# Token rows transposed by copies in SBUF and VectorE blocks instead of TensorE, in a fused attention and mixture-of-experts kernel

## The chip, the cores and the metric

The kernel runs on one core of one Trainium2 chip. The metric is the device time of one launch in microseconds. Three runs of the kernel before gave 1381.59 us as their median (1374.52 to 2207.56).

## The reference, cut to what matters

The input `x` has 4 x 2048 = 8192 tokens of 512 features. All arithmetic is float32.

```
xn  = layernorm(x)                                   # per token, no scale
attn: feats   = exp(xis * (xn @ proj.T) - ...)       # random features, 512 of them
      weights = the same of input_weights            # 512 x 512, made once
      attn    = feats @ weights.T
moe:  score = sigmoid(xn @ router_w)                 # 64 experts
      best 4 of 8 groups, then the best 8 experts, weights normalised, times 2.5
      each expert takes its first 256 tokens: silu(t @ gate) * (t @ up) @ down
      shared expert: silu(xn @ sgate) * (xn @ sup) @ sdown
out = x + attn + moe
```

Every product over the 512 features needs the tokens with features along the partitions, so each group of rows has to be transposed once.

## The kernel before, in words

**Stages.** The kernel has a start (about the first 60 us), a dense stage that goes over 16 groups of 512 tokens, and an expert stage that goes over 64 experts. A float32 product is made of three fp32r matmuls (high times high, low times high, high times low; lines 1034 to 1036), so every operand exists as a high and a low half.

**Start.** SyncE (SP) issues nearly all loads in one queue. Lines 389 to 403 load `xis`, `proj`, `input_weights`, the rows of group 0, the router and the shared expert's gate and up matrices. The last three go through `load_shifted` (lines 333 to 339), which loads a matrix shifted by one row, in three DMAs: three blocks of 128 rows, 127 rows, and one row. VectorE (DVE) then waits for `shared_loaded` (line 922), subtracts the first row from all rows (line 923), and goes on with the low halves, the moments of group 1 and the scores of group 0. TensorE (PE) takes up group 0 behind these.

**Dense stage.** In group g, PE makes 48 matmuls of random features (`dense_dots`), 48 of the shared expert's gate and up, 8 of the next group's router logits, and 72 for the output, in the order of `group` at line 1149. Between them it transposes the next group's normalised rows `xn` in two halves of 8 transposes (`turn_half`, line 1039) into the PSUM tile `ptr`. ScalarE (ACT) copies each half to `xt_hi` (`hi_half`), DVE makes `xt_lo` (`lo_half`). In group g DVE also finds the deviations and normalises group g + 1, and takes the moments of group g + 2 between the outputs 1 and 2 of group g.

**What sets the order.** Each engine's program is written out by hand and waits on semaphores; nothing is planned by a scheduler. SP's order in a group is that of `group` at line 377: the residual rows of group g, x of group g + 2, the store of `xn` of group g + 1 to the table `rows`, then the first half of the output, the router weights and counts of group g + 1, and the second half of the output. A residual is loaded only after the output that lay in the same tile has landed (line 370). The weights of experts 0 and 1 are loaded during the start into `raw[1]` and `raw[0]`.

Of the kernel before, what the change touches and what calls it, by code (L numbers as in the profile page):

```python
# [26 lines left out]
P = 128  # L27
H = 512
# [17 lines left out]
SLOTS = E * CAP  # L46
SPARE = CAP
ROW = H + E
GU = 2 * HB * I
# [38 lines left out]
def build(nc, x, iw, xis, proj, router_w, gate_w, up_w, down_w, sgate_w, sup_w, sdown_w, out):  # L88
    with ExitStack() as ctx:
# [98 lines left out]

        router_raw = gate_a[:, 0:HB * E].rearrange("p (c e) -> p c e", c=HB)
        square = hid  # L190
        iw_raw = raw[1][:, 0:HB * (H + 1)].rearrange("p (c d) -> p c d", c=HB)
# [58 lines left out]
        norm_made = sem("norm_made")  # L250
        xn_stored = sem("xn_stored")
        w_made = sem("w_made")
        w_stored = sem("w_stored")
# [55 lines left out]
        x_groups = x.rearrange("b s h -> (b s) h").rearrange("(g j p) h -> g p j h", j=J, p=P)  # L309
        x_halves = x.rearrange("b s h -> (b s) h").rearrange("(g a j p) h -> g a p j h", a=2, j=2, p=P)  # L310
        rows_groups = rows[0:TOKENS, :].rearrange("(g j p) h -> g p j h", j=J, p=P)
        out_halves = out[0:TOKENS, :].rearrange("(g a j p) h -> g a p j h", a=2, j=2, p=P)
# [9 lines left out]
        def _(sp):  # L322
            def load_x(g):
                sp.dma_start(xbuf[g.b][:], x_groups[g.n]).then_inc(x_loaded[g.b], 16)

            def load_gate_up(b, gate, up):

                sp.dma_start(raw[b][:, 0:GU // 2], gate.rearrange("(p c) i -> p (c i)", p=P)).then_inc(
                    gu_loaded[b], 16)
                sp.dma_start(raw[b][:, GU // 2:GU], up.rearrange("(p c) i -> p (c i)", p=P)).then_inc(  # L330
                    gu_loaded[b], 16)

            def load_shifted(place, source, loaded):
# [14 lines left out]
            def store_xn(g):  # L348
                sp.wait_ge(xn_made, g.n + 1)
                sp.dma_start(rows_groups[g.n][:, :, 0:H], xn[:, :, 0:H]).then_inc(xn_stored, 16)  # L350

            def store_w(g):
# [23 lines left out]

            def group(g, load=True, last=False):
# [6 lines left out]
                if not last:  # L384
                    store_w(g.next())
                    store_counts(g.next())
                store_out(g, 1)
# [25 lines left out]
            sp.wait_ge(iw_sums_turned, 1)  # L413
            load_gate_up(1, gate_w[1], up_w[1])
            load_down(1, down_w[1])
            store_xn(turn(0))
            sp.wait_ge(shared_lo_made, 2)
            load_gate_up(0, gate_w[0], up_w[0])
            load_down(0, down_w[0])
            sp.wait_ge(table_made, 16 * (1 + 2 * SPARE // P))  # L420
# [3 lines left out]
            sp.wait_ge(router_less_made, 1)  # L424
            group(turn(0))
# [4 lines left out]
            group(turn(GROUPS - 2), load=False)  # L430
            load_residual(turn(GROUPS - 1))
# [34 lines left out]
        def _(act):  # L466
# [32 lines left out]
            def hi_half(n, half, dst, psum=ptr):  # L499

                act.wait_ge(turned, 2 * n + half + 1)
                act.activation(dst[:, 2 * half:2 * half + 2, :], psum[:], copy).then_inc(xt_hi_made, 1)

            def sum_signs(n):
# [10 lines left out]
            def group(g, last=False):  # L515
                nxt = g.next()
                for r in range(HB):
                    features(1 + g.n, r, feat_hi)
                if not last:
                    hi_half(nxt.n + 2, 0, xt_hi[nxt.b])  # L520
                hidden(g, 0)
                if not last:
                    hi_half(nxt.n + 2, 1, xt_hi[nxt.b])
# [49 lines left out]
            act.activation(sdn_hi[:], raw[0][:, GU:], copy).then_inc(shared_hi_made, 1)  # L573
            group(turn(0))
            group(turn(1))
# [71 lines left out]
        def _(dve):  # L647
# [23 lines left out]
            def lo_half(n, half, hi, lo, psum=ptr):  # L671
# [3 lines left out]
                    xt_lo_made, 1)  # L675

            def features_lo(s, r, hi, lo, scale=1.0):
                dve.wait_ge(feat_hi_made, HB * s + r + 1)
# [8 lines left out]
            def moments(g):  # L687

                dve.wait_ge(x_loaded[g.b], 16 * (g.i + 1))
                for j in range(J):  # L690
# [23 lines left out]
            def normalise(g, base):  # L714

                dve.wait_ge(turned, 2 * (g.n + 2))
                at_least(dve, xn_stored, 16 * g.n)
                for j in range(J):
# [109 lines left out]
            def group(g, base, before_last=False, last=False):  # L828
# [3 lines left out]
                if not last:  # L832
                    deviations(nxt, base)
                features_lo(1 + g.n, 1, feat_hi, feat_lo)
                if not last:
                    normalise(nxt, base)
                features_lo(1 + g.n, 2, feat_hi, feat_lo)
                features_lo(1 + g.n, 3, feat_hi, feat_lo)
                if last:
                    pass_blocks(0)  # L840
                else:
# [6 lines left out]
            def outputs(g, base, before_last=False, last=False):  # L848

                nxt = g.next()  # L850
                if not last:
# [85 lines left out]
            def first_group(g, base):  # L937
# [11 lines left out]
                weigh(g, base)  # L949
                lo_half(nxt.n + 2, 1, xt_hi[nxt.b], xt_lo[nxt.b])  # L950
                hidden(g, 0, base)
                hidden_lo(g, 0)
# [15 lines left out]
            steps[0] = 0  # L968
            group(turn(GROUPS - 2), start + per_group * (GROUPS - 2), before_last=True)
            steps[0] = 0  # L970
            group(turn(GROUPS - 1), start + per_group * (GROUPS - 1), last=True)

# [57 lines left out]
        def _(pe):  # L1030
# [8 lines left out]
            def turn_half(n, src, half, psum=ptr, free=None):  # L1039
# [3 lines left out]
                for h in range(2):  # L1043
                    for j in range(J):
                        at = 1 + (2 * half + h) * P
                        ins = pe.transpose(psum[:, h, j * P:(j + 1) * P], src[:, j, at:at + P], ident[:])  # L1046
                ins.then_inc(turned, 1)
# [101 lines left out]
            def group(g):  # L1149
                nxt = g.next()  # L1150
                first = isinstance(g.n, int) and g.n == 0
                dense_dots(g, range(1 if first else 0, HB))
                pe.wait_ge(xn_made, nxt.n + 1)
                turn_half(nxt.n + 2, xn, 0)
                if first:
                    pe.wait_ge(shared_lo_made, 1)
                shared_products(g, 0, 0)
                pe.wait_ge(norm_made, nxt.n + 1)
                turn_half(nxt.n + 2, xn, 1)
                if first:  # L1160
                    count(g)
                shared_products(g, 0, 1)
# [34 lines left out]
            pe.transpose(ppos[:, 0:HB], xis_row[:], ident[0:HB, 0:HB]).then_inc(xis_turned, 1)  # L1197
            pe.wait_ge(proj_copied, 1)
            turn_half(0, xn, 0, free=0)
            pe.wait_ge(proj_copied, 2)  # L1200
# [3 lines left out]
            pe.wait_ge(iw_loaded[0], 16)  # L1204
            turn_half(1, iw_raw, 0, psum=pout2, free=0)
            pe.wait_ge(iw_loaded[1], 16)
            pe.wait_ge(pads_made, 1)
            turn_half(1, iw_raw, 1, free=1)
# [11 lines left out]
            for r in range(2, HB):  # L1220
                pe.wait_ge(exp_done, r - 1)
                if r == HB - 1:
                    pe.wait_ge(xn_made, 1)
                    turn_half(2, xn, 0, psum=pout2, free=3)
                    pe.wait_ge(norm_made, 1)
                    turn_half(2, xn, 1, free=4)
# [76 lines left out]
        def _(pool):  # L1303
# [84 lines left out]
            pool.wait_ge(slot_cols_made, 1)  # L1388
            pool.wait_ge(xn_stored, 16 * GROUPS)
            pool.wait_ge(w_stored, 16 * GROUPS)  # L1390
# [40 lines left out]
```

## Time and profile before

| | |
|---|---|
| median of three runs | 1381.59 us |
| time of the profiled execution | 1388.1 us |
| its span, from the first to the last instruction | 1386.4 us |
| mean granted TensorE clock | 0.989 of full speed |
| PE busy | 1333.4 us (96%) |
| DVE busy | 862.1 us (62%) |
| ACT busy | 639.9 us (46%) |
| POOL busy | 480.3 us (35%) |

How to read it: the span is cut into the start, the dense stage (to about 750 us) and the expert stage. A share of busy time is a mean over all three. PE's busy time comes from matmuls that overlap in the trace; the distance between the starts of two of them is what one costs.

### The profile page before, as it was taken

What the parts mean: (1) busy time and instruction counts of PE and PEld (TensorE: products, weight loads), DVE (VectorE), ACT (ScalarE), POOL (GpSimd) and SP (SyncE); (2) the same over time, 40 slices, a digit from 0 to 9 for tenths busy, and PEclk for the clock granted to TensorE, in tenths of its full rate; (3) what the DMA queues carried; (4) which work ended last, traced back from release to release, by engine and by line L of the source; (5) the groups of instructions that cost most, each with busy time, mean ns of one, the idle gap of its engine ahead of it and who ended that gap; (6) DMA issues with size and microseconds to landing.
All of it is one profiled execution on the core that took longest, in us unless ns stands there. A gap on an engine that the chain in (4) does not pass through costs nothing.

```text
span 1386.4 us, 22484 instructions
## 1 busy us (share of the span) xinstructions
PE 1333.4 (96%) x7837; PEld 1165.6 (84%) x7837; DVE 862.1 (62%) x1661; ACT 639.9 (46%) x988; POOL 480.3 (35%) x347
## 2 busy tenths in 40 slices
PE   6899999999999999999999999999999999999994
PEld 5688888888888888888888999999999999888884
DVE  7865755657556575565636676666766666656551
ACT  5311232212322123221236777777777776765662
POOL 1200000000000000000004676877777777555643
PEclk9899999999999999999999999999999999999997
DMA  6351333312333123331217999999999999999895
GB/s 209 128 202 58 106 110 127 108 59 105 107 127 111 61 102 107 127 115 62 68 54 241 263 292 284 280 285 281 288 290 276 295 277 278 260 256 257 240 251 66
DMA packets 117501, 250.00 MB, mean 180 GB/s; under 512 B 31450, under 2 KB 34782, under 8 KB 117470
## 3 DMA queue, kind: packets, MB, share of 16 engines
q1 hardware_dynamic: 88798, 178.28, 38.2%
q0 software_dynamic: 28672, 71.32, 22.7%
q8 instruction: 17, 0.28, 0.1%
q14 instruction: 14, 0.11, 0.0%
HBM read 178.18 MB, written 71.39 MB: 180 GB/s over the span
## 4 chain that ended last, share of the span: by engine, by line
PE 52%; DMA 27%; POOL 9%; issue 6%; DVE 2%; SPq 2%; ACT 1%; DVEq 0%; POOLq 0%; ACTq 0%
DMA out_dram<-outs,slot_cols 24%; PE pmm L1034 9%; PE pmm L1036 9%; PE pmm L1035 9%; POOL out_dram L1383 8%; PE pout L1034 7%; PE pout L1036 6%; PE pout L1035 6%; DMA xbuf<-rows,slot_cols 2%; PE ptr L1046 2%; PE plog L1095 2%; POOL xbuf L1373 2%; SPq L339 1%; PE plog L1104 1%; PE ptr L1249 1%
## 5 line engine op out<-in xcount | busy, mean ns | idle before, releaser
L1383 POOL DMA_INDIRECT out_dram<-outs,slot_cols x128 | 253.3, 1979 | 162.3 <-DMA out_dram<-outs,slot_cols 128.2
L1034 PE MATMUL pmm<-xt_hi,proj_hi 128*128 128x256 f32 (+1 forms) x784 | 253.5, 323 | 4.4 <-DVE xt_lo L989 2.3
L1034 PE MATMUL pmm<-xt_hi,sgu_hi 128*128 128x256 f32 (+1 forms) x768 | 253.1, 330 | 0.0
L1036 PE MATMUL pmm<-xt_hi,proj_lo 128*128 128x256 f32 (+1 forms) x784 | 250.0, 319 | 0.0
L1035 PE MATMUL pmm<-xt_lo,proj_hi 128*128 128x256 f32 (+1 forms) x784 | 250.0, 319 | 0.0
L1036 PE MATMUL pmm<-xt_hi,sgu_lo 128*128 128x256 f32 (+1 forms) x768 | 246.4, 321 | 0.0
L1035 PE MATMUL pmm<-xt_lo,sgu_hi 128*128 128x256 f32 (+1 forms) x768 | 246.2, 321 | 0.0
L1367 POOL TENSOR_TENSOR earlier<-earlier,chosen 128x64 bf16<-128x64 bf16 x64 | 28.6, 446 | 612.0 <-DVE chosen L759 608.2
L1373 POOL DMA_INDIRECT xbuf<-rows,slot_cols x128 | 185.0, 1445 | 91.2 <-DVE slot_cols L802 38.1
L473 ACT ACTIVATE feat<-pmm,ab 128x512 f32<-128x512 f32 x68 | 46.8, 688 | 317.1 <-PE pmm L1036 309.0
L1034 PEld LDWEIGHTS pmm<-xt_hi,proj_hi 128*128 128x128 f32 x784 | 148.3, 189 | 16.1 <-DVE xt_lo L989 2.8
L1036 PEld LDWEIGHTS pmm<-xt_hi,proj_lo 128*128 128x128 f32 x784 | 149.5, 191 | 10.7
L1035 PEld LDWEIGHTS pmm<-xt_lo,proj_hi 128*128 128x128 f32 x784 | 148.1, 189 | 10.5
L1036 PEld LDWEIGHTS pmm<-xt_hi,sgu_lo 128*128 128x128 f32 x768 | 145.9, 190 | 10.9
L1034 PEld LDWEIGHTS pmm<-xt_hi,sgu_hi 128*128 128x128 f32 x768 | 146.5, 191 | 8.8 <-issue 0.2
L1035 PEld LDWEIGHTS pmm<-xt_lo,sgu_hi 128*128 128x128 f32 x768 | 146.1, 190 | 8.9
L983 DVE COPY slot_w<-xbuf 128x2 f32 (+1 forms) x64 | 12.1, 189 | 163.2 <-ACT xt_hi L595 151.8
L612 ACT ACTIVATE outs<-pout,slot_w 128x512 f32<-128x512 f32 x128 | 85.5, 684 | 42.2 <-PE pout L1036 29.5
L1034 PE MATMUL pout<-sdn_hi,hid_hi 128*128 128x512 f32 x256 | 101.4, 396 | 0.0
L1034 PE MATMUL pout<-wt_hi,feat_hi 128*128 128x512 f32 x256 | 101.2, 395 | 0.0
L1036 PE MATMUL pout<-wt_hi,feat_lo 128*128 128x512 f32 x256 | 99.8, 390 | 0.0
L1036 PE MATMUL pout<-sdn_hi,hid_lo 128*128 128x512 f32 x256 | 99.8, 390 | 0.0
(180 smaller groups left out, 2563.5 us busy)
## 6 DMA issues: line engine op xcount, KB each, us to landing
raw<-in_L_ffn_gate_w_dram SPq DMA_DIRECT2D x64, 512.0 KB
raw<-in_L_ffn_up_w_dram SPq DMA_DIRECT2D x64, 512.0 KB
raw<-in_L_ffn_down_w_dram SPq DMA_DIRECT2D x64, 512.0 KB
xbuf<-in_L_attn_x_dram SPq DMA_DIRECT2D x16, 1024.0 KB, 6.4
rows<-xn SPq DMA_DIRECT2D x16, 1024.0 KB, 4.2
outs<-in_L_attn_x_dram SPq DMA_DIRECT2D x32, 512.0 KB, 3.6
out_dram<-outs SPq DMA_DIRECT2D x32, 512.0 KB, 2.9
rows<-weight SPq DMA_DIRECT2D x16, 128.0 KB, 2.8
```

Source lines behind the costliest of these rows:

```text
L339: sp.dma_start(place[P - 1:P, HB - 1], source[0:1]).then_inc(loaded, 16)
L473: act.activation(feat[:, r % 2], pmm[r % 2], ACT.Exp, scale=ab[:, r:r + 1]).then_inc(exp_done, 1)
L612: act.activation(outs[e.b][:, c], pout[c], copy, scale=slot_w[e.q][:, c:c + 1]).then_inc(e_out_made, 1)
L1034: pe.matmul(psum, lh, rh, start=first and n == 0, stop=False)
L1035: pe.matmul(psum, lh, rl, start=False, stop=False)
L1036: ins = pe.matmul(psum, ll, rh, start=False, stop=final and n == len(pairs) - 1)
L1046: ins = pe.transpose(psum[:, h, j * P:(j + 1) * P], src[:, j, at:at + P], ident[:])
L1095: ins = pe.matmul(plog[:], router[:, h, :], part[g.b][:, h, :], start=(h == 0 and part is xt_hi), stop=(h == HB - 1 and part is xt_lo))
L1104: ins = pe.matmul(plog[:, j * E:(j + 1) * E], logits_t[:, j * P:(j + 1) * P], fold[:], start=True, stop=True)
L1367: pool.tensor_tensor(after, earlier[b][:, j, :], chosen[:, j, :], ALU.add).then_inc(earlier_made, 1)
L1373: pool.indirect_dma_start(out=xe[e.b][:, c, :], out_offset=None, in_=rows, in_offset=bass.IndirectOffsetOnAxis(ap=slot_cols[:, at:at + 1], ...
L1383: pool.indirect_dma_start(out=out, out_offset=bass.IndirectOffsetOnAxis(ap=slot_cols[:, at:at + 1], axis=0), in_=outs[e.b][:, c, :], in_of ...
```

## The change

For groups 2 to 15 PE no longer transposes. Instead:

- x is loaded in four DMAs, so that partition 4t + q holds tokens t, t + 32, t + 64 and t + 96 of quarter q of the group (`load_x_quads`). The store of `xn` is in four DMAs in the same way.
- Once group g + 2 is normalised, four DMAs copy `xn` within SBUF: block b of 128 features goes to the quarter of 32 partitions b of the tile `quad` (`load_quad`). A destination partition has 2048 numbers, made of 16 pieces of 128.
- DVE transposes blocks of 32 x 32 from `quad` to `xt_whole`, in two instructions of 1024 columns (`turn_quad`). ACT and DVE take the high and low halves from there.
- Deviations and normalisation of group g + 2 now stand in group g on DVE, between its outputs 1 and 2, and the moments of group g + 2 stand before `hidden(g, 0)`.
- A feature now lies at partition p, block c for feature 4p + c. `load_shifted` loads in that order: 127 partitions with four rows each, then three rows, then one. `turn_half`, still used for `proj`, `input_weights` and groups 0 and 1, reads every fourth column.
- `quad` and `xt_whole` lie in `raw[1]` and `raw[0]`, so the first two experts' weights are loaded in group 14 and no longer during the start.

```diff
 def load_shifted(place, source, loaded):
-    full = (HB - 1) * P
-    sp.dma_start(place[:, 0:HB - 1], source[1:1 + full].rearrange("(c p) i -> p c i", p=P)).then_inc(
+    full = (P - 1) * HB
+    sp.dma_start(place[0:P - 1], source[1:1 + full].rearrange("(p c) n -> p c n", c=HB)).then_inc(loaded, 16)
+    sp.dma_start(place[P - 1:P, 0:HB - 1], source[1 + full:].rearrange("(p c) n -> p c n", p=1)).then_inc(
         loaded, 16)
-    sp.dma_start(place[0:P - 1, HB - 1], source[1 + full:]).then_inc(loaded, 16)
     sp.dma_start(place[P - 1:P, HB - 1], source[0:1]).then_inc(loaded, 16)
...
+def load_x_quads(g):
+    for q in range(P // SQ):
+        sp.dma_start(xbuf[g.b][q:P:P // SQ], x_quads[g.n, q]).then_inc(x_loaded[g.b], 16)
+def load_quad(g):
+    sp.wait_ge(xn_made, g.n + 1)
+    sp.wait_ge(norm_made, g.n + 1)
+    at_least(sp, quad_turned, 2 * (g.n - 2))
+    for b in range(HB):
+        sp.dma_start(quad[b * SQ:(b + 1) * SQ, :], xn[:, :, 1 + b * P:1 + (b + 1) * P]).then_inc(
+            quad_loaded, 16)
...
     load_residual(g)
-    if load:
-        load_x(Turn(g.i + 1, g.b))
-    if not last:
-        store_xn(g.next())
+    if first:
+        store_xn(nxt)
+    else:
+        load_x_quads(later)
     store_out(g, 0)
...
+    store_w(nxt)
+    store_counts(nxt)
+    load_quad(later)
+    store_xn_quads(later)
     store_out(g, 1)
...
+def turn_quad(g, half):
+    dve.wait_ge(quad_loaded, 16 * HB * (g.n - 1))
+    at_least(dve, xt_hi_made, 2 * (g.n - 1 + 2) + 2)
+    at = slice(2 * half, 2 * half + 2)
+    dve.transpose(xt_whole[:, at, :].rearrange("p c (k i) -> p c k i", i=SQ),
+                  quad_blocks[:, at]).then_inc(quad_turned, 1)
...
     features_lo(1 + g.n, 0, feat_hi, feat_lo)
     if not last:
-        deviations(nxt, base)
+        turn_quad(nxt, 0)
+        turn_quad(nxt, 1)
     features_lo(1 + g.n, 1, feat_hi, feat_lo)
     if not last:
-        normalise(nxt, base)
+        lo_quad(nxt, 0)
     features_lo(1 + g.n, 2, feat_hi, feat_lo)
+    if not last:
+        lo_quad(nxt, 1)
     features_lo(1 + g.n, 3, feat_hi, feat_lo)
...
-        lo_half(nxt.n + 2, 0, xt_hi[nxt.b], xt_lo[nxt.b])
-        lo_half(nxt.n + 2, 1, xt_hi[nxt.b], xt_lo[nxt.b])
+    elif not before_last:
+        moments(Turn(g.i + 1, g.b))
     hidden(g, 0, base)
...
-        moments(Turn(g.i + 1, g.b))
+        deviations(later, base)
+        normalise(later, base)
     output(g, 2)
...
     dense_dots(g, range(1 if first else 0, HB))
-    pe.wait_ge(xn_made, nxt.n + 1)
-    turn_half(nxt.n + 2, xn, 0)
     if first:
+        pe.wait_ge(xn_made, nxt.n + 1)
+        pe.wait_ge(norm_made, nxt.n + 1)
+        turn_half(nxt.n + 2, xn, 0)
         pe.wait_ge(shared_lo_made, 1)
     shared_products(g, 0, 0)
-    pe.wait_ge(norm_made, nxt.n + 1)
-    turn_half(nxt.n + 2, xn, 1)
     if first:
+        turn_half(nxt.n + 2, xn, 1)
         count(g)
```

The first place is SP's queue in the start, from the rows of group 0 on (`gate_a` holds the raw router, `raw` the raw shared matrices). Before:

```order
L324 DMA xbuf<-in_L_attn_x_dram 128x4x512
L336 DMA gate_a<-in_L_ffn_router_w_dram 128x3x64
L338 DMA gate_a<-in_L_ffn_router_w_dram 127x64
L339 DMA gate_a<-in_L_ffn_router_w_dram 1x64
L397 DMA outs<-in_L_ffn_router_w_dram 128x64
L336 DMA raw<-in_L_ffn_shared_gate_w_dram 128x3x256
L338 DMA raw<-in_L_ffn_shared_gate_w_dram 127x256
L339 DMA raw<-in_L_ffn_shared_gate_w_dram 1x256
L336 DMA raw<-in_L_ffn_shared_up_w_dram 128x3x256
L338 DMA raw<-in_L_ffn_shared_up_w_dram 127x256
L339 DMA raw<-in_L_ffn_shared_up_w_dram 1x256
L401 DMA outs<-in_L_ffn_shared_gate_w_dram 128x256
```

The same place in the changed kernel:

```order
L332 DMA xbuf<-in_L_attn_x_dram 128x4x512
L349 DMA gate_a<-in_L_ffn_router_w_dram 127x256
L350 DMA gate_a<-in_L_ffn_router_w_dram 1x192
L352 DMA gate_a<-in_L_ffn_router_w_dram 1x64
L439 DMA outs<-in_L_ffn_router_w_dram 128x64
L349 DMA raw<-in_L_ffn_shared_gate_w_dram 127x1024
L350 DMA raw<-in_L_ffn_shared_gate_w_dram 1x768
L352 DMA raw<-in_L_ffn_shared_gate_w_dram 1x256
L349 DMA raw<-in_L_ffn_shared_up_w_dram 127x1024
L350 DMA raw<-in_L_ffn_shared_up_w_dram 1x768
L352 DMA raw<-in_L_ffn_shared_up_w_dram 1x256
L443 DMA outs<-in_L_ffn_shared_gate_w_dram 128x256
```

The number of DMAs is the same; the 127-partition DMA has four times the data, and the 128-partition one is gone.

The second place is SP's queue at the end of a group inside the loop, from the counts on. Before, the output's second half follows them at once:

```order
L359 DMA counts_d<-counts 64x2x128
L374 REGISTER_ALU
L375 DMA out_dram<-outs 128x2x512
L85 REGISTER_ALU
L371 ISA
L371 DMA outs<-in_L_attn_x_dram 128x2x512
```

In the changed kernel:

```order
L385 DMA counts_d<-counts 64x2x128
L367 REGISTER_ALU
L86 ISA
L371 DMA raw<-xn 32x16x128 x4
L376 ISA
L376 DMA rows<-xn 32x4x512
L376 ISA
L376 DMA rows<-xn 32x4x512
...
L400 REGISTER_ALU
L401 DMA out_dram<-outs 128x2x512
```

Eight DMAs, 2 MB in all, stand between the counts and the output's second half (two of the four pairs of L376 are left out here).

## Rows read from the trace of the kernel before

**Rows 1.** Windows: PE, PEld, DVE, ACT, POOL busy us (count); PEclk, DMA share, GB/s.

```profile
90.00:650.00 560.00, 559.85 (x2644) 460.35 (x2643) 345.78 (x935) 138.68 (x208) 23.41 (x52) 1.00 0.30 102
```

**Rows 2.** Timeline of PE in one dense group: start us, us, instruction.

```profile
394.46 0.39 PE L1034 MATMUL pmm<-xt_hi,proj_hi 128*128 128x512 f32 x1
...
405.11 0.39 PE L1036 MATMUL pmm<-xt_hi,proj_lo 128*128 128x512 f32 x1
405.35 1.03 PE L1046 MATMUL ptr<-ident,xn 128*128 128x128 f32 x8
...
406.45 0.40 PE L1035 MATMUL pmm<-xt_lo,sgu_hi 128*128 128x512 f32 x1
...
408.73 0.39 PE L1036 MATMUL pmm<-xt_hi,sgu_lo 128*128 128x512 f32 x1
...
410.29 0.39 PE L1035 MATMUL pmm<-xt_lo,sgu_hi 128*128 128x512 f32 x1
...
414.65 0.39 PE L1034 MATMUL pmm<-xt_hi,sgu_hi 128*128 128x512 f32 x1
...
437.72 0.39 PE L1034 MATMUL pmm<-xt_hi,proj_hi 128*128 128x512 f32 x1
```

**Rows 3.** Chain that ended last, the start stage: start us, us, what.

```profile
24.25 5.76 DMA outs<-n_L_ffn_shared_up_w_dram
...
62.00 0.53 PE pmm L1034
```

**Rows 4.** Timeline of DVE in the start; in brackets the idle time before it.

```profile
30.03 2.29 DVE L669 TENSOR_TENSOR raw<-raw,outs 128x2048 f32<-128x2048 f32 x1 [2.18 <-DMA outs<-n_L_ffn_shared_up_w_dram]
```

**Rows 5.** Timeline of SP in the start: start us, us in its queue.

```profile
6.42 6.10 SPq L339 DMA_DIRECT2D gate_a<-in_L_ffn_router_w_dram  x1
...
18.54 5.27 SPq L339 DMA_DIRECT2D raw<-n_L_ffn_shared_up_w_dram  x1
```

**Rows 6.** Windows of the start, columns as in Rows 1.

```profile
21.80:23.60 1.80, 1.19 (x5) 0.45 (x4) 1.49 (x11) 0.86 (x2) 0.00 (x0) 1.00 0.07 24
48.50:50.50 2.00, 2.00 (x11) 1.65 (x10) 1.97 (x4) 0.70 (x2) 0.00 (x0) 1.00 1.02 414
```

**Rows 7.** Timeline of DVE in the same dense group.

```profile
399.46 0.18 DVE L698 BATCH_NORM_AGGREGATE mean_var<-stats 128x2 f32<-128x6 f32 x1
...
402.06 0.16 DVE L711 SCALAR_TENSOR_TENSOR rstd<-rstd 128x4 f32<-128x4 f32 x1
...
402.95 1.91 DVE L719 TENSOR_SCALAR xn<-xbuf,mean_var,rstd 128x512 f32<-128x512 f32 x4
...
407.84 1.23 DVE L674 TENSOR_TENSOR xt_lo<-ptr,xt_hi 128x1024 fp32r<-128x1024 f32 x1 [0.22 <-ACT xt_hi L502]
...
413.17 0.69 DVE L813 SCALAR_TENSOR_TENSOR hid<-gate_a,pmm 128x512 f32<-128x512 f32 x1
...
430.04 0.41 DVE L777 TENSOR_SCALAR counts<-ppos 128x256 bf16<-128x256 f32 x1
430.37 2.46 DVE L691 BATCH_NORM_STATS2 stats<-xbuf 128x6 f32<-128x512 f32 x4
```

**Rows 8.** Timeline of ACT in the same group.

```profile
402.82 0.69 ACT L473 ACTIVATE feat<-pmm,ab 128x512 f32<-128x512 f32 x1 [1.37 <-PE pmm L1036]
```

**Rows 9.** Timeline of SP at the group's end.

```profile
439.29 2.96 SPq L371 DMA_DIRECT2D outs<-in_L_attn_x_dram  x2
442.44 0.37 SPq L324 DMA_DIRECT2D xbuf<-in_L_attn_x_dram  x1
```

**Rows 10.** Page, part 6: DMA issues, KB each, median us from issue to landing.

```profile
xbuf<-in_L_attn_x_dram SPq DMA_DIRECT2D x16, 1024.0 KB, 6.4
rows<-xn SPq DMA_DIRECT2D x16, 1024.0 KB, 4.2
...
out_dram<-outs SPq DMA_DIRECT2D x32, 512.0 KB, 2.9
rows<-weight SPq DMA_DIRECT2D x16, 128.0 KB, 2.8
```

More of the change, by code:

```diff
@@ L310, in build @@
         x_halves = x.rearrange("b s h -> (b s) h").rearrange("(g a j p) h -> g a p j h", a=2, j=2, p=P)
+        x_quads = x.rearrange("b s h -> (b s) h").rearrange("(g q j t) h -> g q t j h", q=P // SQ, j=J, t=SQ)
+        rows_quads = rows[0:TOKENS, :].rearrange("(g q j t) h -> g q t j h", q=P // SQ, j=J, t=SQ)
         rows_groups = rows[0:TOKENS, :].rearrange("(g j p) h -> g p j h", j=J, p=P)
@@ L350, in store_xn, with store_xn_quads @@
                 sp.dma_start(rows_groups[g.n][:, :, 0:H], xn[:, :, 0:H]).then_inc(xn_stored, 16)
+            def load_quad(g):
[5 more added lines that the diff above has]
+                        quad_loaded, 16)
+            def store_xn_quads(g):
+                for q in range(P // SQ):
+                    sp.dma_start(rows_quads[g.n, q][:, :, 0:H], xn[q:P:P // SQ, :, 0:H]).then_inc(xn_stored, 16)
             def store_w(g):
@@ L375, in store_out, with group, before_last_group @@
                 sp.dma_start(out_halves[g.n, a], outs[a][:]).then_inc(out_stored[a], 16)
-            def group(g, load=True, last=False):
+            def group(g, first=False):
+                nxt, later = g.next(), Turn(g.i + 1, g.b)
                 load_residual(g)
-                if load:
-                    load_x(Turn(g.i + 1, g.b))
-                if not last:
-                    store_xn(g.next())
+                if first:
+                    store_xn(nxt)
+                else:
+                    load_x_quads(later)
                 store_out(g, 0)
-                if not last:
-                    store_w(g.next())
-                    store_counts(g.next())
+                store_w(nxt)
+                store_counts(nxt)
+                load_quad(later)
+                store_xn_quads(later)
+                store_out(g, 1)
+            def before_last_group(g):
+                nxt = g.next()
+                load_residual(g)
+                sp.wait_ge(quad_turned, 2 * (GROUPS - 2))
+                load_gate_up(1, gate_w[1], up_w[1])
+                load_down(1, down_w[1])
+                sp.wait_ge(xt_lo_made, 2 * (GROUPS + 2))
+                load_gate_up(0, gate_w[0], up_w[0])
+                load_down(0, down_w[0])
+                store_out(g, 0)
+                store_w(nxt)
+                store_counts(nxt)
                 store_out(g, 1)
@@ L424, in _ @@
             sp.wait_ge(router_less_made, 1)
-            group(turn(0))
+            group(turn(0), first=True)
             group(turn(1))
@@ L429, in _ @@
                     group(Turn(i, b))
-            group(turn(GROUPS - 2), load=False)
+            before_last_group(turn(GROUPS - 2))
             load_residual(turn(GROUPS - 1))
@@ L502, in hi_half, with hi_quad @@
                 act.activation(dst[:, 2 * half:2 * half + 2, :], psum[:], copy).then_inc(xt_hi_made, 1)
+            def hi_quad(g, half):
+                act.wait_ge(quad_turned, 2 * (g.n - 2) + half + 1)
+                act.wait_ge(up_done, IB * (g.n - 1))
+                at = slice(2 * half, 2 * half + 2)
+                act.activation(xt_hi[g.b][:, at, :], xt_whole[:, at, :], copy).then_inc(xt_hi_made, 1)
             def sum_signs(n):
@@ L513, in sum_signs, with group @@
                     ins.then_inc(signs_summed, 1)
-            def group(g, last=False):
+            def group(g, first=False, last=False):
                 nxt = g.next()
-                for r in range(HB):
-                    features(1 + g.n, r, feat_hi)
-                if not last:
+                features(1 + g.n, 0, feat_hi)
+                features(1 + g.n, 1, feat_hi)
+                if not first and not last:
+                    hi_quad(nxt, 0)
+                features(1 + g.n, 2, feat_hi)
+                if not first and not last:
+                    hi_quad(nxt, 1)
+                features(1 + g.n, 3, feat_hi)
+                if first:
                     hi_half(nxt.n + 2, 0, xt_hi[nxt.b])
                 hidden(g, 0)
-                if not last:
+                if first:
                     hi_half(nxt.n + 2, 1, xt_hi[nxt.b])
@@ L573, in _ @@
             act.activation(sdn_hi[:], raw[0][:, GU:], copy).then_inc(shared_hi_made, 1)
-            group(turn(0))
+            group(turn(0), first=True)
             group(turn(1))
@@ L714, in normalise @@
             def normalise(g, base):
-                dve.wait_ge(turned, 2 * (g.n + 2))
-                at_least(dve, xn_stored, 16 * g.n)
+                if isinstance(g.n, int) and g.n <= 2:
+                    dve.wait_ge(turned, 2 * (g.n + 2))
+                    at_least(dve, xn_stored, 16 * g.n)
+                else:
+                    dve.wait_ge(quad_loaded, 16 * HB * (g.n - 2))
+                    dve.wait_ge(xn_stored, 32 + 16 * (P // SQ) * (g.n - 2))
                 for j in range(J):
@@ L848, in outputs @@
             def outputs(g, base, before_last=False, last=False):
-                nxt = g.next()
+                nxt, later = g.next(), Turn(g.i + 1, g.b)
                 if not last:
@@ L950, in first_group @@
                 lo_half(nxt.n + 2, 1, xt_hi[nxt.b], xt_lo[nxt.b])
+                moments(Turn(g.i + 1, g.b))
                 hidden(g, 0, base)
@@ L968, in _ @@
             steps[0] = 0
-            group(turn(GROUPS - 2), start + per_group * (GROUPS - 2), before_last=True)
+            start += per_group * (GROUPS - 2)
+            group(turn(GROUPS - 2), start, before_last=True)
+            start += steps[0]
             steps[0] = 0
-            group(turn(GROUPS - 1), start + per_group * (GROUPS - 1), last=True)
+            group(turn(GROUPS - 1), start, last=True)
             def down_lo(e):
@@ L1044, in turn_half @@
                     for j in range(J):
-                        at = 1 + (2 * half + h) * P
-                        ins = pe.transpose(psum[:, h, j * P:(j + 1) * P], src[:, j, at:at + P], ident[:])
+                        block = src[:, j, 1 + 2 * half + h::HB]
+                        ins = pe.transpose(psum[:, h, j * P:(j + 1) * P], block, ident[:])
                 ins.then_inc(turned, 1)
@@ L1203, in _ @@
             turn_six(less3).then_inc(less_turned, 1)
-            pe.wait_ge(iw_loaded[0], 16)
+            for half in range(2):
+                pe.wait_ge(iw_loaded[half], 16)
+            pe.wait_ge(pads_made, 1)
             turn_half(1, iw_raw, 0, psum=pout2, free=0)
-            pe.wait_ge(iw_loaded[1], 16)
-            pe.wait_ge(pads_made, 1)
             turn_half(1, iw_raw, 1, free=1)
```

28 lines of the change are left out of this document (17 added, 11 removed).

## The prediction

> **What bounds the kernel now.** I read the windows first, then PE's own timeline, then the chain and the queues of the start. In the dense stage PE is busy 559.85 of 560 us at the full granted clock, without a wait [rows 1]. So there every matmul or transpose taken from PE is a gain in full, as long as what replaces it keeps up. One group lasts 43.26 us, from the matmul that opens it at 394.46 us to the one at 437.72 [rows 2]. The expert stage behind it issues the same instructions before and after, and I leave it out. In the start it is another matter: DVE waits 2.18 us for the last load of the shared matrices, which lands at 30.03 us [rows 3, 4], and from there a chain of work, mostly DVE's, leads to the matmul at 62.00 us with which PE takes up group 0 in earnest [rows 3]. A later landing moves everything behind it by the same time.
>
> **The transposes (gain).** In rows 2 two matmuls of 0.23 us each lie between the start of L1036 at 405.11 and the start of L1035 at 406.45. That is 1.34 us, of which 0.46 are the matmuls; 0.88 belong to the 8 transposes and the changes to and from them. The second half: 410.29 - 408.73 - 0.46 = 1.10 us. Together 1.98 us per group. Groups 2 to 15 lose them, 14 groups: **-27.7 us**.
>
> **The loads of the start (loss).** The changed `load_shifted` moves 127 partitions x 4 rows in one DMA. What does a DMA of 127 partitions cost? Between 21.80 and 23.60 us, while SP stands in the next one-row DMA (18.54 us, 5.27 long [rows 5]) and the 127-row DMA of a shared matrix is under way, the DMA share is 0.07 and the rate 24 GB/s [rows 6]: one of sixteen engines, where 16 give 414 GB/s in the same start [rows 6]. So 127 partitions go through one engine. Bytes on it before: 127 x 256 B for the router and 2 x 127 x 1024 B for gate and up, 292.6 KB (thousands of bytes). After: 127 x 1024 B and 2 x 127 x 4096 B, 1170.4 KB. Off goes its sixteenth of the three-block loads (884.7 KB / 16 = 55.3 KB). Net 822.5 KB more, in order, on one engine. At 24 GB/s that is 34.3 us; at 414 / 16 = 25.9 GB/s, the rate with packets of 4 KB, 31.8 us. I take the second, since the new pieces have that size: **+31.8 us**. The landing moves from 30.0 to about 62 us, and PE's start of group 0 from 62 to about 94 us. Bounds: below, a gain of 2.2 us, if the DMA is spread over all engines after all (DVE's whole idle time there [rows 4]); above, 37 us, if the queue of SP, which stood 6.10 us and 5.27 us in one-row DMAs behind such loads [rows 5], also holds back the loads behind for one more such stop.
>
> The Trainium skill ("DMA: Bandwidth & Descriptors", section "Why a DMA increments its semaphore by 16 and not by 1") says that a DMA runs on the largest number of engines up to 16 that divides the slowest dimension of both sides, and names 127 partitions as a case of one. By that rule the two big loads stay on one engine, as in the sum; the trace agrees, with 24 GB/s. This rule speaks against the change.
>
> The other edits of the start cost nothing that shows: PE waits for both halves of `proj` and `input_weights` before it turns them (a microsecond or two), and the router's rows come later, both long before 62 us; without that cover they would be on DVE's chain. Six DMAs of expert weights, 3 MB, leave the start and come in group 14; SP has some 25 us there between the new waits and the first output, and the copies need about 8 us at 414 GB/s [rows 6]. The moments of group 2 (2.46 us [rows 7]) now stand before `hidden(0, 0)` on DVE, where in group 0 the up product is waited for anyway.
>
> **What replaces the transposes.** DVE gets two transposes of 1024 columns. The trace has none. A subtraction of 1024 columns takes 1.23 us [rows 7]; half of it if two elements went per cycle, twice it if the blocks need two passes. I take 1.23 each. They stand in the place of the deviations (399.46 to 402.22, 2.76 us [rows 7]), so DVE is not later there; with 2.46 each it would be 2.2 us later, which the 43 us of a group with 0.62 busy on DVE take in. ACT copies the two high halves between exponentials, where it idles 1.37 us [rows 8]; a copy of 1024 columns should take it no longer than DVE's subtraction, 1.23. Both cost nothing, with PE's wait for the exponential two steps later as cover.
>
> The critical part is the **DMA chain**. Set the next group's start at 437.72. DVE ends the counts at 430.45, then the deviations (2.76) and the normalisation (402.95 to 405.14, 2.19) end at 435.4 [rows 7]. Only then does SP issue four copies, four stores of `xn`, and the second output store, which stood right behind the counts before. All run in order on the same engines. From issue to landing 512 KB take 2.9 us and 1 MB 4.2 us [rows 10]: 1.3 us for 512 KB, with 1.6 us fixed. The 2048 pieces of 512 B of the copy have no row. By bytes alone they take 2.6 us; by the router weights' pieces of 256 B (512 of them in 2.8 - 1.6 = 1.2 us [rows 10]) 4.8 us. Middle 3.7. The output store then lands at 435.4 + 1.6 + 3.7 + 2.6 + 1.3 = 444.6, with 443.5 and 445.7 as ends. For that landing the next residual load waits, and behind it stands x of the group after. Before, that residual was issued at 441.85 [rows 9], and x landed at 442.44 + 6.4 = 448.8 [rows 9, 10], 7.0 us later. So x lands at 451.6 (450.5 to 452.7).
>
> Who needs it? DVE's moments now stand before `hidden`, 2.46 us, then two operations of 0.69 us and about 0.2 between them, 4.0 in all [rows 7]; PE needs their result where L1034 stood at 414.65 [rows 2], in the next group at 457.91, less 1.98 for the transposes: 455.9. So x may land at 451.9 at the latest. The middle fits by 0.3 us; at the upper end 0.8 us are lost in each of 13 groups, 10 us. I set down **+1 us**, and keep 0 to +10. The copies themselves land by 435.4 + 1.6 + 3.7 = 440.7, DVE wants them at 442.7: no wait.
>
> The Trainium skill (same page, section "Why small descriptors are slow (HBM only)") says that copies within SBUF don't suffer from small pieces as HBM does. By it the copy would be near its lower end, and x would be in time in every group; no run here shows it yet.
>
> **Sum.** 1388.1 (the profiled execution) - 27.7 + 31.8 + 1.0 = 1393.2. The median of the runs shown is 1381.6, 0.5% below that execution; the difference of +5.1 set on the median gives **1387 us**. Range of this case alone: 1378 to 1399.
>
> **The rivals.**
> 1. *x comes too late* (slower). If a piece of 512 B costs as much as one of 2 KB (2.6 us / 512 each), the copy takes 10.4 us instead of 3.7, x lands at 458.3, 6.4 us after the last moment, and 13 groups lose 83 us: 1470. It decides from a copy of 4.0 us on; each further microsecond costs 13. To be slower by over 2% (27.6 us) it takes a copy of about 5.8 us. For it: a margin of 0.3 us, and eight issues of SP in a row. Against: the 256 B stores, that give 4.8. Typical 1392 to 1425.
> 2. *The big loads don't clog one engine*, or something else waits there anyway (faster). Then only the gain is left: 1381.6 - 27.7 - 2.2 + 1 = 1353. For it: nothing in the rows but that the source is one unbroken run. Against: the 127-row load before also was one, at 24 GB/s.
> 3. *Nothing gained on PE*: the freed time turns up as a wait for the high halves on ACT, with the loss in the start kept: 1381.6 + 31.8 = 1413. The margins above speak against it.
>
> **Chances.** My forecast 0.60; rival 1 0.26 (0.18 of it under 1409, 0.08 above); rival 2 0.11; rival 3 0.03. A measurement of this kernel tells about 2%, 27.6 us, from no change, so faster means below 1354 and slower above 1409. Faster 0.09, within 2% 0.80, slower 0.11. The range leaves out rival 2 and the cases above 1409, some 2 in 10: 1366 to 1409.
>
> **What would show it.** PE's timeline in a steady group: 41.3 us from group to group and no idle row. Right for the start: the wait of DVE for the shared matrices ends near 62 us, with a window of some 40 us at 25 GB/s and share 0.06. Rival 1: idle PE with `hid` as releaser in each group, and idle DVE before the moments, released by x. Rival 2: the shared matrices there before 30 us. I am wrong on the whole if the dense stage speeds up by 27.7 us and the start does not grow, or if the copy takes over 4 us.

## The result, and the profile after

The changed kernel is slower: four runs gave a median of 1472.75 us (1445.34 to 1510.27), where four of the kernel before gave 1378.09. Executions of one kernel come in a faster and a slower state, whatever the kernel, and every ratio here compares the faster ones alone: it is 1.0585, with a 95% interval of 1.043 to 1.0739. The forecast was 1387 with a range up to 1409. The profiled execution took 1445.34 us, its span is 1443.6.

The page after: PE busy, the slices of PE and of its granted clock, and the DMA issues (KB each, median us to landing), to be read beside [rows 1, 10].

```profile
PE 1325.9 (92%) x7613; PEld 1157.8 (80%) x7613; DVE 913.1 (63%) x1689; ACT 636.3 (44%) x988; POOL 493.0 (34%) x347
...
PE   6299988899889988899899999999999999999995
...
PEclk9599989999999999999999999999999999999998
...
xbuf<-in_L_attn_x_dram SPq DMA_DIRECT2D x56, 256.0 KB, 3.9
raw<-xn SPq DMA_DIRECT2D x56, 256.0 KB, 6.2
rows<-xn SPq DMA_DIRECT2D x56, 256.0 KB, 7.2
```

PE has its 224 transposes fewer (7613 instead of 7837 matmuls), yet is no longer full in the dense stage (the 8s in its row), and a copy of 256 KB takes longer to land than 1 MB of `xn` did before.

Where the time went is read off best at the first transpose of the expert stage, the end of the dense one. Its line in the kernel before, then after (ns min/median/max, first and last start in us):

```profile
L1249 PE MATMUL ptr<-ident,xbuf x512: 270/283/421, 735.1 to 1348.1; 128*128 128x128 f32 x171
```

```profile
L1323 PE MATMUL ptr<-ident,xbuf x512: 270/283/386, 809.8 to 1407.7; 128*128 128x128 f32 x171
```

The dense stage ends at 809.8 instead of 735.1 us: +74.7. The expert stage, from there to the end of the span, has the same instructions and took 1386.4 - 735.1 = 651.3 us before and 633.8 here. In the other profiles it lies between 633 us (copy_halves) and 683 us (two_queues), and no run shows why. So whole times can differ by tens of us for a reason that lies behind the dense stage, and below I compare the end of the dense stage, in one profile per kernel.

**The start.** DVE's row after, for [rows 4], and SP's queue, for [rows 5]:

```profile
58.75 2.29 DVE L720 TENSOR_TENSOR raw<-raw,outs 128x2048 f32<-128x2048 f32 x1 [29.96 <-DMA outs<-n_L_ffn_shared_up_w_dram]
```

```profile
13.39 10.65 SPq L350 DMA_DIRECT2D raw<-L_ffn_shared_gate_w_dram  x1
...
25.01 12.56 SPq L350 DMA_DIRECT2D raw<-n_L_ffn_shared_up_w_dram  x1
37.61 6.95 SPq L352 DMA_DIRECT2D raw<-n_L_ffn_shared_up_w_dram  x1
```

```profile
25.50:37.00 11.50, 7.64 (x39) 5.72 (x37) 3.26 (x8) 4.14 (x6) 0.00 (x0) 0.96 0.07 28
```

The window (columns as in [rows 6]) shows a DMA share of one engine in sixteen, at 28 GB/s, while the big loads run; it stays so until SP gets on to the loads behind them at 44.60 us. The shared matrices land at 58.75 us instead of 30.03: +28.7.

**The dense stage.** PE in one group after, for [rows 2]; SP, DVE and a window of the same group:

```profile
404.00 0.39 PE L1109 MATMUL pmm<-xt_hi,proj_hi 128*128 128x512 f32 x1
...
415.98 0.50 PE L1109 MATMUL pmm<-xt_hi,sgu_hi 128*128 128x512 f32 x1 [0.95 <-ACT feat L511]
...
426.50 0.50 PE L1109 MATMUL pmm<-xt_hi,sgu_hi 128*128 128x512 f32 x1 [2.96 <-DVE hid L882]
...
449.69 0.39 PE L1109 MATMUL pmm<-xt_hi,proj_hi 128*128 128x512 f32 x1
```

```profile
350.56 1.53 SPq L385 DMA_DIRECT2D counts_d<-counts  x2
...
397.69 1.53 SPq L385 DMA_DIRECT2D counts_d<-counts  x2
402.02 2.77 SPq L371 DMA_DIRECT2D raw<-xn  x4
404.98 3.07 SPq L376 DMA_DIRECT2D rows<-xn  x4
408.25 0.45 SPq L401 DMA_DIRECT2D out_dram<-outs  x1
408.96 7.20 SPq L397 DMA_DIRECT2D outs<-in_L_attn_x_dram  x2
416.34 3.11 SPq L337 DMA_DIRECT2D xbuf<-in_L_attn_x_dram  x4
```

```profile
412.19 3.89 DVE L733 STREAM_TRANSPOSE raw<-raw 128x1024 f32<-128x1024 f32 x2 [3.12 <-DMA raw<-xn]
...
422.67 2.47 DVE L756 BATCH_NORM_STATS2 stats<-xbuf 128x6 f32<-128x512 f32 x4 [2.54 <-DMA xbuf<-in_L_attn_x_dram]
```

```profile
404.00:411.00 7.00, 7.00 (x32) 5.82 (x31) 1.39 (x2) 2.64 (x4) 0.00 (x0) 1.00 1.25 135
412.00:414.00 2.00, 2.00 (x11) 1.65 (x10) 1.81 (x1) 0.00 (x0) 0.00 (x0) 1.00 1.05 406
```

The group shown lasts 449.69 - 404.00 = 45.69 us, where 41.3 was forecast and 43.26 was the value before; the one ahead of it, from counts to counts, 397.69 - 350.56 = 47.13 us. The copies begin at 402.02 and run at 135 GB/s until 411, with all engines taken; at 412 the stores behind them run at 406 GB/s. Everything in SP's queue follows: the residual loads, the second of which waits for the output to land, keep SP for 7.20 us, x is issued at 416.34 and holds DVE until 422.67, `hid` is late, PE waits 2.96 us. A smaller wait of 0.95 us comes through the transposes and the exponential. By the waits table, from 130 to 700 us PE waits 37.8 us for `hid` and 10.3 us for `feat`, 12 times each:

```profile
PE pmm L1109 <- DVE hid L882: 37.8, 12, 4.9
PE pmm L1109 <- ACT feat L511: 10.3, 12, 0.9
```

Over the whole dense stage (100 to 760 us) it is 40.8 us in 13 groups for `hid` and 11.4 us in 14 groups for `feat`:

```profile
PE pmm L1109 <- DVE hid L882: 40.8, 13, 4.9
PE pmm L1109 <- ACT feat L511: 11.4, 14, 0.9
```

On top of the waits the clock's mean falls. Windows of the same stretch, before and then after (columns as in [rows 1]):

```profile
130.00:700.00 570.00, 569.83 (x2687) 468.59 (x2686) 345.57 (x935) 138.67 (x208) 23.41 (x52) 1.00 0.29 99
```

```profile
130.00:700.00 570.00, 521.92 (x2267) 423.44 (x2267) 367.21 (x892) 126.46 (x195) 19.24 (x48) 0.96 0.46 116
```

The granted clock goes from 1.00 to 0.96 in a stage whose PE now pauses. It does not fall after every pause. Windows of 1 us from 130 to 700 us show ten stretches at half clock (1.2 GHz), 41.0 us together, one at each of ten of the 13 waits for `hid`; the other three waits, that of the group shown among them, have none. One such stretch, behind a wait of 2.90 us that ended at 379.24, as a window and in PE's rows, where the starts lie 0.43 us apart instead of 0.23:

```profile
381.00:384.00 3.00, 3.00 (x11) 2.71 (x12) 1.02 (x2) 0.38 (x1) 0.00 (x0) 0.50 0.00 0
```

```profile
382.82 0.63 PE L1110 MATMUL pmm<-xt_lo,sgu_hi 128*128 128x512 f32 x1
383.25 0.63 PE L1111 MATMUL pmm<-xt_hi,sgu_lo 128*128 128x512 f32 x1
```

Later groups with such a stretch last 47.1 to 47.6 us from counts to counts, those without 45.6. One of the ten stretches is three times as long as the others and stands at the longest wait, 4.88 us; its group lasts 51.88 us. From these lengths I estimate the cost of the lower clock at some 19 us in all.

### The profile page after: what moved, and what is told of

Its sections match the earlier page's. It is cut to its first block, busy times and chain, and to the rows that moved or that the text cites. A ratio compares the mean times of both kernels' runs of the same rounds, so it can differ in the third digit from the quotient of the medians.

```text
span 1443.6 us, 22418 instructions
## 1 busy us (share of the span) xinstructions
PE 1325.9 (92%) x7613; PEld 1157.8 (80%) x7613; DVE 913.1 (63%) x1689; ACT 636.3 (44%) x988; POOL 493.0 (34%) x347
## 4 chain that ended last, share of the span: by engine, by line
DMA 34%; PE 27%; SPq 11%; DVE 10%; POOL 9%; issue 8%; ACT 1%; DVEq 0%; POOLq 0%; ACTq 0%
DMA out_dram<-outs,slot_cols 21%; POOL out_dram L1457 8%; DMA out_dram<-outs 7%; PE pmm L1109 5%; PE pmm L1111 4%; PE pmm L1110 4%; PE pout L1109 4%; PE pout L1111 4%; PE pout L1110 4%; DMA xbuf<-in_L_attn_x_dram 4%; SPq L376 3%; SPq L371 3%; SPq L350 2%; SPq L337 2%; DVE stats L756 2%
## 5 line engine op out<-in xcount | busy, mean ns | idle before, releaser
L1109 PE MATMUL pmm<-xt_hi,sgu_hi 128*128 128x256 f32 (+1 forms) x768 | 258.1, 336 | 52.2 <-DVE hid L882 40.8
L1457 POOL DMA_INDIRECT out_dram<-outs,slot_cols x128 | 259.6, 2028 | 128.3 <-DMA out_dram<-outs,slot_cols 98.7
L1111 PE MATMUL pmm<-xt_hi,sgu_lo 128*128 128x256 f32 (+1 forms) x768 | 250.0, 326 | 0.0
L1110 PE MATMUL pmm<-xt_lo,sgu_hi 128*128 128x256 f32 (+1 forms) x768 | 249.9, 325 | 0.0
L1447 POOL DMA_INDIRECT xbuf<-rows,slot_cols x128 | 194.0, 1515 | 92.6 <-DVE slot_cols L871 38.1
```

The costliest lines, as they stand in the source:

```text
L1109: pe.matmul(psum, lh, rh, start=first and n == 0, stop=False)
L1110: pe.matmul(psum, lh, rl, start=False, stop=False)
L1111: ins = pe.matmul(psum, ll, rh, start=False, stop=final and n == len(pairs) - 1)
L1447: pool.indirect_dma_start(out=xe[e.b][:, c, :], out_offset=None, in_=rows, in_offset=bass.IndirectOffsetOnAxis(ap=slot_cols[:, at:at + 1], ...
L1457: pool.indirect_dma_start(out=out, out_offset=bass.IndirectOffsetOnAxis(ap=slot_cols[:, at:at + 1], axis=0), in_=outs[e.b][:, c, :], in_of ...
```

## The experiments

In all of them A is the changed kernel. "Dense end" is the first expert transpose, 735.1 us before and 809.8 in A. dev_early, two_queues and the four copy_ runs are one execution each; of them only the trace is read. In the four copy_ runs a wrong matrix is transposed and the exponential's scale is a hundredth, so that they show times and no result.

**start_only.** The kernel before, with A's start alone.

```diff
-    full = (HB - 1) * P
-    sp.dma_start(place[:, 0:HB - 1], source[1:1 + full].rearrange("(c p) i -> p c i", p=P))...
-    sp.dma_start(place[0:P - 1, HB - 1], source[1 + full:])...
+    full = (P - 1) * HB
+    sp.dma_start(place[0:P - 1], source[1:1 + full].rearrange("(p c) n -> p c n", c=HB))...
+    sp.dma_start(place[P - 1:P, 0:HB - 1], source[1 + full:].rearrange("(p c) n -> p c n", p=1))...
...
-    at = 1 + (2 * half + h) * P
-    ins = pe.transpose(psum[:, h, j * P:(j + 1) * P], src[:, j, at:at + P], ident[:])
+    block = src[:, j, 1 + 2 * half + h::HB]
+    ins = pe.transpose(psum[:, h, j * P:(j + 1) * P], block, ident[:])
```

> The kernel before with only the new order of the start: load_shifted by 127 partitions of four rows, turn_half with every fourth column, and PE's waits for both halves of proj and input_weights. The dense stage keeps its transposes on TensorE. Theory A (the 127-partition loads go through one DMA engine, and this is a cost of its own beside the copies): the shared matrices land near 58 us instead of 30, as in the changed kernel (58.75), the dense stage runs 43.3 us per group as before, and the time is 28 to 30 us over the kernel before, near 1407. Rival B (most of the 57 us between the two profiled spans comes from the dense stage, and a late start is taken back behind it): under 10 us more than before.

Measured: shared matrices used at 58.91 us, dense end at 763.8, +28.7 on the kernel before. The dense stage waits nowhere. Theory A holds: the start is a cost of its own, and nothing behind takes it back. (Whole times, 1398.84 and 1399.13, stand 30 us over the mean of 1369.4 of the kernel before, 1364.71 to 1379.19, measured beside them.)

**start_spread.** A, with its 127 rows cut where the engines divide them.

```diff
-    sp.dma_start(place[0:P - 1], source[1:1 + full]...
+    cut = 112
+    sp.dma_start(place[0:cut], source[1:1 + cut * HB]...
+    sp.dma_start(place[cut:P - 1], source[1 + cut * HB:1 + full]...
```

> The changed kernel, with each 127-partition load cut into one of 112 partitions and one of 15. Theory A: 112 and 15 rows go through 16 and 15 engines, the shared matrices land at 28 to 32 us, DVE's wait of 30.0 us falls to about 2, and the kernel is 26 to 30 us shorter than the changed one, whose dense stage stays at 47 us per group. Rival B: the source being one unbroken run is what puts the load on one engine; then the landing stays near 58 us and nothing is gained.

Measured: DVE takes the shared matrices at 29.14 us without a wait, dense end at 783.5, 26.3 us before A's. The ratio to the kernel before is 1.0365 (1.0292 to 1.0438): the rest of the loss is in the dense stage. The source is as unbroken as in A, so it is the count of rows that matters. This also is what the trace of before had shown with 24 GB/s [rows 6].

**x_first.** A, with `load_x_quads(later)` ahead of `load_residual(g)`.

> The changed kernel, with the loads of x for group g + 2 issued before the residual loads of group g, so that x no longer waits for the landing of the output store of the group before. Theory C (PE's waits for hid, 2.96 us in the group at 404 us and 40.8 us in all, come from x landing late): DVE's wait before the moments vanishes, PE's wait for hid with it; what is left is the wait of 0.95 us for the exponential, and the group falls from 47.2 to some 42.5 us, 50 to 65 us less in all. Rival D (the copies within SBUF themselves set the pace, since their late landing holds DVE before the transposes): DVE's wait moves, the group falls by 2 us at most, under 30 us in all.

Measured: dense end at 759.4, 50.4 us before A's; PE's waits from 130 to 700 us:

```profile
PE pmm L1109 <- ACT feat L511: 11.4, 14, 0.9
PE pmm L1109 <- DVE hid L882: 4.5, 13, 0.4
```

Theory C holds: a group takes 43.0 us (42.5 was expected). The wait for `hid` was x's lateness and all but goes; the wait for the exponential stays, since the copies are as slow as before (6.2 us to landing). The clock comes back with it: none of these pauses is over 0.95 us, and the mean from 130 to 700 us is 1.00, with no stretch at half clock. The ratio to the kernel before is 1.0183 (1.009 to 1.0276): the dense end is still 24.3 us behind the kernel before, less than the start's 28.7.

**dev_early.** A, with `deviations(later)` moved from between the outputs to behind `hidden_lo(g, 0)`.

> The changed kernel, with the deviations of group g + 2 moved before the scores, where VectorE idles some 2 us, so that the copies start 2.7 us earlier. Theory C (after the start, the group's length is set by when the copies are done, through x and through the high halves): everything behind moves by 2.7 us, PE's wait for the exponential (0.95) vanishes, that for hid falls from 3 to under 0.5 us, and a group takes 43 us instead of 47.2. Rival H: the scores come later by as much as is saved, and the group stays above 46 us.

Measured: dense end at 775.6, 34.2 us before A's. PE's wait for the exponential is gone, that for `hid` falls to 23.2 us in 13 groups, 1.8 each and not under 0.5, and a new one for `hid_lo` (9.3 us) comes up. A group takes 44.3 us and not 43. The copies' start counts, as theory C has it; its figure was too hopeful, x is still behind the same queue. Two stretches at half clock are left, 6.8 us together.

**copy_wide.** A, with the copies going straight across.

```diff
-    sp.dma_start(quad[b * SQ:(b + 1) * SQ, :], xn[:, :, 1 + b * P:1 + (b + 1) * P])
+    at = min(1 + b * P, H - P)
+    sp.dma_start(quad[:, b * H:(b + 1) * H], xn[:, :, at:at + P])
```

> The changed kernel, with the four copies of xn within SBUF going straight across: 128 partitions to the same 128 partitions, 512 B pieces as before and the same bytes. What is transposed is then not the matrix that the reference needs, and the scale of the exponential is taken as a hundredth, so that numbers stay finite: the computation is changed, the work is not. Theory E (the copies run at 130 GB/s, 77 ns per packet of 512 B, because each writes to 32 partitions only): they run at 250 GB/s or more and 1 MB is done in about 4 us, the wait for hid vanishes. Rival F (pieces of 512 B between two places in SBUF cost 77 ns wherever they go): the rate stays at 130 GB/s.

Measured: 3.1 us from issue to landing instead of 6.2, dense end at 742.8, 67.0 us before A's. A window from 2 to 4 us after the first copy's issue:

```profile
369.79:371.79 2.00, 2.00 (x10) 1.68 (x9) 0.69 (x1) 0.00 (x0) 0.00 (x0) 1.00 1.00 285
```

The piece of 512 B is not slow. With copies at 285 GB/s PE waits 6.3 us in 12 groups, and the dense stage, less A's start, is 742.8 - 28.7 = 714.1, or 21.0 us shorter than before.

**copy_1k.** A, with pieces of 1 KB to the same quarters: the source is `xn[:, 0:2, 1:1 + 2 * P]` for each b.

> The changed kernel, with copies that take pieces of 1 KB in place of 512 B, to the same quarters of 32 partitions and with the same bytes; the matrix that is transposed is then another one, and the exponential's scale is taken as a hundredth, so the computation is changed. Theory E (the destination limits): 130 to 150 GB/s, 6 us to landing, as with 512 B. Rival F (the small piece limits): twice the rate, 3 to 4 us to landing.

Measured: 6.2 us to landing, as with 512 B, dense end at 812.3, and in the same window of a group

```profile
357.02:359.02 2.00, 2.00 (x11) 1.65 (x10) 0.69 (x1) 0.00 (x0) 0.00 (x0) 1.00 1.13 132
```

Rival F is out: the size of the piece does not decide. That the destination does is shown by copy_strided below.

**two_queues.** A, with the copies for b = 2 and 3 issued by ScalarE at the end of its group.

> The changed kernel, with the copies to quarters 0 and 1 issued by SyncE and those to quarters 2 and 3 by ScalarE, so that both run at once; the same pieces, the same bytes, the reference's result. Theory E, sharper after copy_wide (6.2 us from issue to landing against 3.1): what limits is the quarter of the partitions that a copy writes, so two at once on different quarters go at 200 GB/s or more, 1 MB in 4 to 5 us instead of 7.5, and DVE's wait before the transposes (36.4 us in 12 groups) falls under 10 us. Rival G (copies within SBUF from all partitions to fewer are limited by the engines' own work per piece, whatever runs beside them): 130 GB/s stays and the wait too.

```profile
353.47:355.47 2.00, 2.00 (x11) 1.65 (x10) 0.69 (x1) 0.00 (x0) 0.00 (x0) 1.00 1.26 129
```

A miss for theory E: two quarters at once go at 129 GB/s together. The waits before the transposes fall from 36.4 to 27.2 us only, dense end at 801.8. Rival G's number holds, its reason does not, as the next one shows.

**copy_strided.** A, with each copy to every fourth partition: `quad[b:P:P // SQ, :]` in place of `quad[b * SQ:(b + 1) * SQ, :]`.

> The changed kernel, with each copy going to 32 partitions as before, but to every fourth partition of all 128 (b, b + 4, b + 8, ...) instead of a quarter next to each other. The matrix that is transposed is another one, and the exponential's scale is a hundredth: the computation is changed. Both copy_1k (pieces twice as long: still 6.2 us to landing) and two_queues (two quarters at once: still about 130 GB/s) are behind. Theory J (what counts is which partitions one copy writes: a quarter lies behind few of the paths into SBUF): 250 GB/s or more, 3 to 4 us to landing, as in copy_wide. Theory K (what counts is how few partitions each engine writes, 2 in a copy, whichever they are): 130 GB/s and 6 us as before.

```profile
368.50:370.50 2.00, 2.00 (x10) 1.68 (x9) 0.69 (x1) 0.00 (x0) 0.00 (x0) 1.00 1.01 287
```

3.1 us to landing, dense end at 741.1. The source (but for a shift by one column at b = 3), the pieces and the count of 32 partitions are A's, and the rate is twice as high: theory J, which partitions are written, and not K.

**copy_halves.** A, with two copies to 64 neighbouring partitions each.

> The changed kernel, with two copies of 512 KB, each to 64 partitions next to each other, in pieces of 1 KB; the matrix is another one and the exponential's scale a hundredth. Theory J: if the paths of 64 neighbours are as few as those of 32, the rate stays at 130 GB/s; if they are twice as many, 260. Theory K: 4 partitions per engine instead of 2, so 260 GB/s.

```profile
360.21:362.21 2.00, 2.00 (x11) 1.65 (x10) 0.69 (x1) 0.00 (x0) 0.00 (x0) 1.00 1.11 116
```

116 GB/s for 64 neighbours, and 106 in the 2 us behind: no more than for 32. The dense end is 820.4. Theory K is out a second time.

The Trainium skill ("SBUF — State Buffer", section "Door 1: The DMA port swizzle") says that partitions 0 to 31 and 0 to 63 both lie behind the same 8 of 16 ports. The same page of the Trainium skill, section "Can I just issue two DMAs to hit both halves?", says that two DMAs on different halves hardly help each other. The order of all five copy runs agrees. Half the ports should give half the rate: half of the 285 to 287 GB/s of the copies that write across all 128 partitions is 143, and the runs show 106 to 135. Half of the 406 GB/s of the stores would be 203; copies within SBUF did not reach it.

**all_mended** and **all_mended_again.** start_spread, x_first and dev_early together, the copies left slow.

> The changed kernel with the 127-partition loads cut in 112 and 15, x loaded before the residuals, and the deviations moved early: three mends together. If start and copies are the whole of the loss, PE waits for nothing in the dense stage, a group takes 41.3 us, the granted clock there is 1.00, and the time is 25 to 30 us under the kernel before, 1340 to 1345. Rival: the transposes and copies cost PE in another way still (contention with its reads, a wait that comes next), and the gain is under 15 us.

> The same kernel as all_mended (its start, its order of x and of the deviations mended), to be told from the kernel before by more rounds. Its first profile had the dense stage end 22.9 us earlier than in the kernel before, and PE waiting 2.4 us in 12 groups. Theory: the whole is faster by 15 to 27 us, a ratio of 0.981 to 0.989. Rival: the two are the same within 0.5%, because the expert stage takes back what the dense stage gave.

Measured: dense end at 712.2 and 712.1 us, 22.9 and 23.0 before the kernel before. Over its counts rows a group takes 41.7 us. PE in the dense stage of the second:

```profile
130.00:650.00 520.00, 517.43 (x2345) 423.97 (x2344) 374.16 (x899) 135.41 (x203) 19.02 (x48) 1.00 0.53 136
```

The ratio to the kernel before is 0.9826 (0.9776 to 0.9877) in the second run: faster than the kernel before by 1.7%, clear of noise though under the 2% of the prediction, and so faster than A too. The 25 to 30 us that the first expected were too much, the 15 to 27 of the second hold. What lacks from 27.7 is in part a wait of 0.2 us per group for `hid_lo`; the rest, some 2 us, was not traced. The copies still run at some 130 GB/s; they are merely off the path.

## Why the prediction was wrong

- **Transposes, -27.7 us: right.** all_mended has 23.0 of it with one small wait left, at 41.7 us per group against 41.3.
- **Start, +31.8 us: right.** start_only shows +28.7. The 127-row DMAs went at one engine's share, 28 GB/s and not 25.9. That SP would be held up by one-row DMAs was true too, 10.65 and 12.56 us, but by the rows it lay beside the load; no run tried it alone.
- **DVE's transposes, 1.23 us each: mis-sized.** They take 3.89 us for two. This was within the bound set (2.46 each), and lies in the chain that ends in the wait for the exponential; what it adds there was not tried alone.
- **The copies: the step that failed.** The prediction put 1 MB at 3.7 us, with 2.6 and 4.8 as ends, from the bytes and from stores of 256 B pieces. They took 412.1 - 402.0 - 1.6 = 8.5 us. Both ends asked what a piece costs; neither asked which partitions one DMA writes, and the rows used for them had 128 partitions each. So the upper end was no bound. What the Trainium skill says of copies within SBUF ("DMA: Bandwidth & Descriptors", section "Why small descriptors are slow (HBM only)") was true of the piece size (512 B and 1 KB ran alike, and 512 B at 285 GB/s in copy_wide) and beside the point.
- **The chain behind them: right.** The prediction had x as the one in need, a limit of 4.0 us for the copies, and 13 us for each further one: (8.5 - 4.0) x 13 = 58 us. The group shown bears it out: 45.69 - 41.3 = 4.4 us lost. They come as two waits, though, 40.8 us for `hid` and 11.4 us for the exponential, 52.2 in all; the second the prediction had excluded, because it had the copies landed 2.0 us before DVE wants them.
- **The clock: a term put at nothing.** The dense stage lost 809.8 - 735.1 - 28.7 + 27.7 = 73.7; copy_wide gives 67.0 of it back. The two waits are 52.2 of it, the stretches at half clock some 19 by my estimate. The forecast's 83 us for rival 1 had no such term either. The last 2 to 3 us were not traced.
- **Chances.** Rival 1 is what came, with 0.26, of which 0.08 beyond the range: x too late, at a price of up to 83 us. Its reason, a piece of 512 B that costs as much as one of 2 KB, was not the cause; that its 10.4 us for the copies lie near the measured 8.5 is luck. A margin of 0.3 us under a duration that no row showed did not bear 0.60 on the other side.

## What to carry to other kernels

For a DMA that reads or writes part of the partitions, take the price from a row with the same set of partitions, or treat the rate as open by a factor of three. Before work is taken off the busiest engine, lay out the queue that feeds its replacement, down to the last load behind it: here the cure was to put x ahead of a load that waits for a landing. Loads of 127 rows went at one engine's rate; cut in 112 + 15 they cost nothing that showed. And where work leaves the busiest engine, count with its clock: a wait that replaces the work can cost more than its length.

## What the runs showed of the hardware

- Copies within SBUF to 32 or 64 neighbouring partitions ran at 106 to 135 GB/s, to 32 partitions spread over all 128 or to all 128 at 285 to 287, with 512 B pieces. Two issuing queues did not change the first.
- A DVE transpose of 128 x 1024 float32 in 32 x 32 blocks took 1.95 us, 1.6 times a subtraction of that size.
- Ten of the 13 waits for `hid` in A (2.7 to 4.9 us) came with a stretch at the lower of the clock's two levels, three did not; the mean granted clock from 130 to 700 us went from 1.00 to 0.96. In dev_early a wait of 1.84 us had such a stretch too. In x_first, with waits of 0.95 us at most, the clock stayed at 1.00 throughout. A stretch cost 1.5 us or more: groups of 47.1 us and more instead of 45.6.

Why copies within SBUF stop at 285 GB/s where stores ran at 406, and why 64 neighbours got less than 32, stays open.
